# Causal mask of the low scores as a minimum on VectorE, and maxima turned by ordinary products

## What is computed

```python
h = edges(x)                                  # 16 images, (256, 256)
h = h + attn(layernorm(h), ...)
h = h + layernorm(h) @ sign(weight).T
# attn: 16 heads of 16 columns, 256 positions
scores = einsum('bqhd,bkhd->bhqk', Q, K) / 4
scores = where(causal, scores, -inf)
attn = softmax(scores, axis=-1)
out = einsum('bhqk,bkhd->bqhd', attn, V) @ W_o
```

## Time and profile before

| | |
|---|---|
| median of 3 runs | 418.94 us (417.73 to 421.58) |
| the profiled execution | 420.82 us |
| its span, first to last instruction | 419.0 us |
| mean granted TensorE clock | 0.975 of 2.4 GHz |
| TensorE busy | 379.0 us, 90% |
| VectorE busy | 290.5 us, 69% |
| ScalarE busy | 239.7 us, 57% |
| GpSimd busy | 168.3 us, 40% |

### The profile page before, as it was taken

How to read it: one execution, slowest core, us unless ns; L and a number is a source line. 1 busy time by engine, 2 the same in 40 slices (tenths; PEclk the granted TensorE clock), 3 DMA queues, 4 the chain that set the end, 5 groups by cost and what they waited for, 6 DMA issues and landing times.

```text
span 419.0 us, 10082 instructions
## 1 busy us (share of the span) xinstructions
PE 379.0 (90%) x3667; PEld 261.4 (62%) x3667; DVE 290.5 (69%) x551; ACT 239.7 (57%) x410; POOL 168.3 (40%) x359
## 2 busy tenths in 40 slices
PE   2967867788999999999999999999999998979985
PEld 0432445556676767676777767676767675757663
DVE  3225543778777877787878686878786868767751
ACT  2125343766675848494848485767674756353631
POOL 8000050547363626263636363636452432321221
PEclk9977996999999999999999999999999999989999
DMA  6984978688787878869696969798666261610001
GB/s 191 213 175 130 225 186 256 184 206 214 228 220 231 247 210 230 231 170 265 164 265 152 253 173 251 187 232 201 180 170 176 61 181 59 197 58 28 7 22 52
DMA packets 72283, 74.14 MB, mean 177 GB/s; under 512 B 6403, under 2 KB 66091, under 8 KB 72235
## 3 DMA queue, kind: packets, MB, share of 16 engines
q1 hardware_dynamic: 70506, 72.71, 65.0%
q10 hardware_dynamic: 1729, 0.80, 0.8%
HBM read 51.98 MB, written 21.04 MB: 174 GB/s over the span
## 4 chain that ended last, share of the span: by engine, by line
PE 63%; DMA 15%; SPq 8%; DVE 6%; issue 3%; ACT 2%; POOL 1%; POOLq 0%; ACTq 0%; DVEq 0%
PE bank L1020 13%; PE bank L1151 7%; PE bank L1084 7%; PE bank L1113 6%; SPq L344 5%; DMA gray_padded<-gray 4%; PE bank L1034 4%; DMA x_sb<-in_x 4%; DMA qk_parts<-parts 4%; PE bank L1069 3%; PE bank L1050 3%; PE bank L1013 3%; PE bank L1086 3%; PE bank L1115 3%; PE bank L1130 3%
## 5 line engine op out<-in xcount | busy, mean ns | idle before, releaser
L662 ACT ACTIVATE probs<-bank 128x1024 f32<-128x1024 f32 x64 | 65.1, 1017 | 49.4 <-PE bank L1115 48.5
L856 DVE TENSOR_REDUCE top<-bank 128x4 f32<-128x1024 f32 x64 | 78.0, 1219 | 21.2 <-PE bank L1086 21.1
L866 DVE TENSOR_TENSOR bank<-bank,cap_kq 128x512 f32<-128x512 f32 x64 | 44.7, 698 | 27.1 <-PE bank L1130 24.6
L1084 PE MATMUL bank<-k_st,q_st 96*128 96x256 bf16 x256 | 46.8, 277 | 6.4 <-DMA k_st<-qk_parts 4.9
L1113 PE MATMUL bank<-q_st,k_st 99*128 99x256 bf16 x256 | 47.1, 278 | 1.7 <-DMA q_st<-top_rows 1.7
L1151 PE MATMUL bank<-probs,v_ring 128*32 128x256 f32 x512 | 41.3, 394 | 4.8 <-DVE rest L849 3.2
L861 DVE TENSOR_REDUCE top<-bank 128x4 f32<-128x512 f32 x64 | 41.6, 650 | 0.0
L667 ACT ACTIVATE probs<-bank 128x512 f32<-128x512 f32 x64 | 38.0, 594 | 2.0 <-DVE bank L866 1.9
L481 POOL TENSOR_SCALAR var<-mv 128x2 f32<-128x2 f32 x16 | 3.6, 225 | 84.4 <-DVE mv L907 84.4
L1115 PE MATMUL bank<-mask_kq,ident_bf 128*128 128x256 bf16 x128 | 35.6, 278 | 0.0
L873 DVE STREAM_TRANSPOSE u<-bank 128x256 f32<-128x256 f32 x64 | 28.7, 448 | 9.7 <-PE bank L1154 4.5
(11 more groups left out here) (109 smaller groups left out, 766.3 us busy)
## 6 DMA issues: line engine op xcount, KB each, us to landing
x_sb<-in_x SPq DMA_DIRECT2D x16, 768.0 KB, 5.4
rows<-gray_padded SPq DMA_DIRECT2D x48, 256.0 KB
qk_parts<-parts SPq DMA_DIRECT2D x48, 256.0 KB, 3.2
q_st<-qk_parts SPq DMA_DIRECT2D x96, 128.0 KB, 3.4
k_st<-qk_parts SPq DMA_DIRECT2D x96, 128.0 KB, 3.4
gray_padded<-gray SPq DMA_DIRECT2D x16, 258.0 KB, 3.8
out_dram<-z SPq DMA_DIRECT2D x15, 256.0 KB, 2.9
rows<-gray_padded SPq DMA_DIRECT2D x32, 24.0 KB
```

The source lines that it names most:

```text
L662: nc.scalar.activation(probs[:, g, :, 0:S], ps_k0, ACT.Exp, scale=SCALE).then_inc(exp0_done, 1)
L856: nc.vector.tensor_reduce(top[:, 1, g // 2, :, g % 2], ps_hi, AX.X, ALU.max, negate=True).then_inc(max_hi_done, 1)
L866: nc.vector.tensor_tensor(ps_k1, ps_k1, cap_kq[:, :].unsqueeze(1).to_broadcast([P, G, P]), ALU.min).then_inc(capped, 1)
L1084: nc.tensor.matmul(ps_hi[:, i, :], q[:, hh, P:S], k[:, hh, :], start=(i == b * two), stop=False, skip_group_check=True)
```

## The change

- The mask product L1099 is gone for all four groups (`LO_MIN = (0, 1, 2, 3)`); the four score products each stand alone, and the last signals `lo_done`.
- VectorE takes the minimum of the low scores in bank 2 with a new f32 tile `cap_qk` (3e38 at or below the diagonal, -3e38 above) in a new step `cap_lo`, one instruction of 128x512, right behind `max_hi` of the same group. It signals `lo_capped`, for which `max_lo` waits.
- In stage 1 `max_lo(i, 1)` moves behind `turn_attn(i - 2, 1)` (and in iteration 1 behind `turn_values` and `rest_of_gray(4)`).
- `turn_max` uses ordinary products with the identity, into f32, instead of transposes into bf16.
- GpSimd draws one more tile (memset and select) before TensorE's first products.

```diff
+LO_MIN = (0, 1, 2, 3)
+        cap_qk = sb("cap_qk", [P, P])
-        ps_mt = bank[:, 5, :].bitcast(BF16)
+        ps_mt = bank[:, 5, :]
...
+                pool.affine_select(out=cap_qk[:, :], in_=cap_qk[:, :], compare_op=ALU.is_ge, fill=MASK,
+                                   base=0, pattern=[[-1, P]], channel_multiplier=1).then_inc(drawn, 1)
...
+            pool.memset(cap_qk[:, :], -MASK).then_inc(cleared, 1)
...
             def max_lo(n, g):
-                dve.wait_ge(lo_done, NG * n + g + 1)
+                if g in LO_MIN:
+                    dve.wait_ge(lo_capped, len(LO_MIN) * n + LO_MIN.index(g) + 1)
+                else:
+                    dve.wait_ge(lo_done, NG * n + g + 1)
                 nc.vector.tensor_reduce(top[:, 0, g // 2, :, g % 2], ps_lo, AX.X, ALU.max,
                                         negate=True).then_inc(max_lo_done, 1)
+
+            def cap_lo(n, g):
+                dve.wait_ge(lo_done, NG * n + g + 1)
+                nc.vector.tensor_tensor(ps_lo, ps_lo, cap_qk[:, :].unsqueeze(1).to_broadcast([P, G, P]),
+                                        ALU.min).then_inc(lo_capped, 1)
...
                 if live(i):
                     max_hi(i, 0)
+                    cap_lo(i, 0)
...
                     max_hi(i, 1)
-                    max_lo(i, 1)
+                    cap_lo(i, 1)
                 if i == 1:
                     turn_values(0, 0)
                     rest_of_gray(4)
                 if live(i - 2):
                     turn_attn(i - 2, 1)
+                if live(i):
+                    max_lo(i, 1)
...
                     max_hi(i, 2)
+                    cap_lo(i, 2)
...
                     max_hi(i, 3)
+                    cap_lo(i, 3)
...
                 need(pe, max_lo_done, NG * n + g)
+                if g in LO_MIN:
+                    for i in range(G):
+                        hh = g % 2 + 2 * i
+                        last = nc.tensor.matmul(ps_lo[:, i, :], q[:, hh, 0:P], k[:, hh, 0:P],
+                                                start=True, stop=True)
+                    last.then_inc(lo_done, 1)
+                    return
...
-                    last = nc.tensor.transpose(ps_mt[0:PARTS * HALF, t * P:(t + 1) * P],
-                                               top_parts[:, t, :, :].rearrange("p c h -> p (c h)"),
-                                               ident_bf[:, :])
+                    last = nc.tensor.matmul(ps_mt[0:PARTS * HALF, t * P:(t + 1) * P],
+                                            top_parts[:, t, :, :].rearrange("p c h -> p (c h)"),
+                                            ident_bf[:, :], start=True, stop=True)
```

More of the change, by code:

```diff
@@ L261, in build @@
         capped = sem("capped")
+        lo_capped = sem("lo_capped")
         exp0_done = sem("exp0_done")
@@ L444, in draw_masks @@
             def draw_masks():
-                pool.wait_ge(cleared, 7)
+                pool.wait_ge(cleared, 8)
                 for m in (ident, ident_bf):
@@ L545, in _ @@
             pool.memset(v_ring[:, :, :, :, DK:VW], 1.0).then_inc(ones_set, 1)
-            pool.wait_ge(drawn, 2 * TAPS + 5)
+            pool.wait_ge(drawn, 2 * TAPS + 6)
             pool.wait_ge(ones_set, 1)
@@ L557, in _ @@
                     sum_edges(i + 2)
+                if live(i + 2):
                     scale_x(i + 2)
@@ L1208, in keep_warm @@
                     nc.tensor.matmul(bank[:, 5, :], ident_bf[:, :], mask_qk[:, :, :], start=True, stop=True)
-            pe.wait_ge(drawn, 2 * TAPS + 5)
+            pe.wait_ge(drawn, 2 * TAPS + 6)
             keep_warm(36)
```

## The result

The changed kernel takes 424.9 us (median of 6 executions, 422.7 to 426.3) against 419.0 us before (6 executions): ratio 1.015, 95% interval 1.011 to 1.019. It is slower by 5.9 us; 1.5 us had been forecast, and 424.9 lies just outside the range.

A forecast was written before the change was run, and what follows sets the result against it. The loop was taken as bound by TensorE for about 17.3 us, then VectorE for 4.36 us. Loop +1.32, ramp -0.2 and tail +0.34 made +1.46 us on the median 418.94: forecast 420.4 us, range 416.5 to 424.8.

The forecast's parts named there:

- Two legs, the second set by VectorE: Loop period: about 17.3 us bound by TensorE up to group 3's high scores, then 4.36 us bound by VectorE, becoming 4.96.
- V: TensorE's instruction values(i - 2, 3), which opens iteration i behind the first key scores; said to wait for VectorE's two subtractions.
- The rival "gain": TensorE sets the whole loop period, so all four removed mask products count: 411 us, chance 0.10.
- The mask products: TensorE, groups 0 to 2: removal saves 0.16 us each, 0.48 an image, with 0.11 us of f32 load exposed; group 3 nothing.
- the rival "even": The f32 loads on TensorE stay hidden, so the first leg gains 0.66 us an iteration: 418.4 us, chance 0.12.
- The minimum's price and the tight spot: VectorE: each minimum takes 0.60 us; tightest in group 0, with 0.85 us left before TensorE wants the bank for lo_scores(i, 1).
- The rival "slower": VectorE and GpSimd disturb each other, cap_lo(i, 0) loses 1.1 us and delays lo_scores(i, 1): 423.7 us, chance 0.15.
- The maxima by ordinary products: Turns of maxima on TensorE become ordinary products: zero cost, bound 0.05 us an image either way.
- Loop +1.3: Iterations 4 to 14: 11 x (0.60 - 0.48) = +1.3 us, minimum added less mask products saved.
- ramp -0.2: Start, before the gray sum at 76.33: reduction exchanged for minimum, a half-clock mask product goes, a load takes back half: -0.2 us.
- tail +0.34: End: VectorE behind group 3 twice on the chain, +1.2 us, against TensorE's savings in iterations 14 and 15: +0.34 us.
- the granted clock only as a gain: Rival: ordinary products for the maxima keep TensorE at 2.4 GHz from 65 to 70 us: 417.9 us, chance 0.03.

The follow-up runs named there:

- the other orders: Changed kernel, subtractions ahead of group 3's minimum: in all iterations 1.0052, 421.3 us; minima and order for images 3 to 13 only, xn_t copied early, 0.9874, 413.5 us.
- The early copy: Changed kernel with ScalarE copying xn_t ahead of scaling the colours: ratio 1.0048 to the kernel before, median of all ten executions 422.9 us.
- ramp, loop or tail alone: Changed kernel with minima only for images 0 to 2, 3 to 13, or 14 and 15, mask products elsewhere: 1.0043, 1.0094, 1.0029 of the kernel before.
- filling the gap of iteration 14: Changed kernel with twelve unused 512-column products on TensorE ahead of values of iteration 14: ratio 1.0139 to the kernel before, 425.3 us.

## Why the prediction was wrong

*Two legs, the second set by VectorE: right.* The reduction of group 3 to V was forecast at 4.96 us and is 4.96 in every period; taking that minimum out brings 4.36 back, and it alone raises the period by 0.60. The wait before V was to be 0.9 us put down to the subtractions; it is 0.70 in the profile's count in ten iterations and 2.71 in iteration 14. It is shorter than the sum had it because group 3's mask product freed TensorE of 0.07 us only, not 0.22: `filters` then waits for the same reduction of group 3 (in the changed kernel that ends at 218.84, and `filters` starts at 218.94). This is why TensorE's own second leg came out at 4.18 us in the other orders and not at 4.0. The rival "gain" had nothing to it.

*The mask products: the mechanism as stated was wrong, the size nearly right by luck.* I took 0.11 us of an f32 load to be exposed behind each group, 0.48 us saved in all. The loads hide wholly. The low scores before, then in the changed kernel with the f32 turn behind them:

```profile
202.12 0.39 PE L1097 MATMUL bank<-k_st,q_st 96*128 96x128 bf16 x4
```
```profile
202.14 0.39 PE L1118 MATMUL bank<-k_st,q_st 96*128 96x128 bf16 x4
202.37 0.61 PE L1033 MATMUL bank<-ident,yn 128*128 128x128 f32 x4
```

0.23 us apart, where 0.44 lay between the two before (202.12 to 202.56); in groups 1 and 2 it is 0.22 in place of 0.44. So 0.21 to 0.22 a group was freed, 0.65 in all, as the rival "even" had it. The Trainium skill, page "TensorE: Matmul & The Clock Gate", section "Back-to-back issue gap", gives about 216 ns for an isolated product of 512 columns; the trace agrees, and the 0.65 us, an estimate worked out from it, was nearer than my 0.48. ScalarE took back what I had wrongly subtracted: `values` of group 1 needs the copy of xn_t, and that copy stands behind ScalarE's other work, not behind TensorE. Copy and product, before and after:

```profile
209.63 0.59 ACT L619 COPY xn_t<-bank 128x512 f32<-128x512 f32 x1
210.41 0.64 PE L1151 MATMUL bank<-probs,v_ring 128*32 128x256 f32 x8
```
```profile
209.49 0.58 ACT L626 COPY xn_t<-bank 128x512 f32<-128x512 f32 x1
210.22 0.64 PE L1178 MATMUL bank<-probs,v_ring 128*32 128x256 f32 x8
```

Where the product waits for the copy it follows 0.14 to 0.15 us behind its end, as it does after the change (210.07 and 210.22). Before, it followed 0.19 behind (210.22 and 210.41), so the slack was some 0.05 us. With two mask products gone TensorE is there 0.43 us sooner, the copy ends only 0.16 sooner against V, and the rest is waited for. The turn that the copy reads was done by 207.9 and 207.5, so it doesn't wait for TensorE. I had looked for covers of waits on VectorE only, and named none on ScalarE. Net 0.40 in place of 0.48: +0.20 us a period in place of +0.12, 0.9 us of the miss. The early copy shows it: 16.72.

*The minimum's price and the tight spot: right.* 0.60 us as `cap`; no wait of TensorE on the low maxima in the loop. The rival "slower" by contention falls: 64 minima average 689 ns, no more than `cap`. The Trainium skill, page "SBUF — State Buffer", section "SBUF: two separate sides", lets GpSimd block a VectorE instruction only in a two-port mode or with two inputs in SBUF, and `cap_lo` has one; the trace agrees.

*The maxima by ordinary products: right, zero.* The extra tile lets TensorE's first product start at 8.52 us in place of 8.11; whether that costs anything at the end was not measured alone.

*Loop +1.3, ramp -0.2: the terms of the sum that failed, and tail +0.34, which is not proven wrong.* Measured alone, the loop's images cost 3.9 us (2.8 to 5.1), the ramp's 1.8 (0.3 to 3.3) and the tail's 1.2 (0 to 2.5, which doesn't exclude 0.34). Of the loop's 2.6 us over the forecast the traces show 0.9, the copy's; the other 1.7 are open. Of the ramp I had only counted what stands ahead of one gray sum, and what its 1.8 us are made of is open. Two things were missing. I worked out the ends from one trace, and in the ends one trace is a draw: V of iteration 3 came between 109.7 and 115.7 us in the traces taken, and the two profiled executions of before and after happened to have 112.5 and 112.6. And I had the granted clock only as a gain. Where TensorE waits longer for VectorE in a gap, it can come out of it at 1.2 GHz: iteration 14 idled 1.90 us before (low clock behind it in three of six traces with that gap) and 2.71 after (low in all four whose gap was not filled), and one such stretch cost 1.55 us. Since the gap of iteration 14 hangs on the minimum of image 13, that stretch counts as the loop's. Over the executions timed, the mean granted clock was 0.973 to 0.976 before (three groups of 23 to 29 executions) and 0.966 after (6), with ramp, loop or tail alone 0.968 to 0.970: some 7 us more of the 420 at half clock after the whole change. How much of what the periods don't explain (3 to 4 us of the 5.9) this makes is not settled. Within these groups of before the time rises by 0.5 to 1.3 us for each 0.01 of clock, which would give about 1 us; filling the gap of iteration 14 gave nothing that could be told from the noise. The rest stays open.

*The range.* Its upper end left out the last tenth of the forecast case; bounds on ramp and tail of +0.3 and +1.0 were too tight for what no row bounded (1.8 and 1.2 were measured).

## What to carry to other kernels

When work moves from a full engine to a half-idle one, look for the one place in the loop where the full engine waits for the other: an instruction there costs its whole length each time round, whatever the shares of busy time say; the same instruction a few places on is free. Where a wait hangs on a chain through other engines, speeding up the engine that waits only uncovers it, so read the slack of each such chain, ScalarE's too. And try a rearrangement made for the loop without ramp and tail: the same minima and order gave +0.5% when written for all iterations, and, held to the loop with one copy moved as well, -1.3%. How much of that each of the steps makes was not measured.

## What the runs showed of the hardware

Weight loads of f32 operands hid behind four bf16 products of 128 columns each: nothing was left to see of them (0.23 us from the first such product to the f32 one, of which the four take 4 x 0.055 us). The granted clock of a single core is far from a constant of the kernel: executions of the kernel before had means of 0.960 to 0.988. TensorE's idle gap of 1.9 us ahead of V of iteration 14 was followed by a stretch with 1.2 GHz in three traces and not in three others; behind a gap of 2.7 us in the same place it came in all four, and cost 1.55 us where it was worked out (the changed kernel). The minimum of 128x512 with scores in PSUM and one f32 tile in SBUF takes 0.69 us on record and 0.60 us from its start to its neighbour's.
